# A recurrence step that multiplies by the decay where TensorE left it

## The chip, the cores and the metric

One core of a Trainium2 chip runs the whole program. The metric is device time in microseconds (us), from the core's own record of an execution; lower is better. The engines are TensorE (PE, with its weight loads as PEld), VectorE (DVE), ScalarE (ACT), GpSimd (POOL) and SyncE (SP), which only issues DMAs here.

## The reference

The input `x` is 4 batches of 1024 tokens with 256 channels. It is layer-normed to `xn`, and two parts work on `xn`:

```python
# state-space part: per batch a state h of 256 channels x 16 states
dA = exp(soft_clamp(dt * A)); dB = dt * B            # dt, B, C: projections of xn
h = dA[t] * h + dB[t] * x[t]
h = h * min(20 / norm(h), 1)                          # norm over the whole state of a batch
s[t] = einsum('bdn,bn->bd', h, C[t]) + Dp * x[t]
# expert part: 8 experts, top 2 of each token, capacity 1280
f = combine(gelu(dispatch(xn) @ c_fc) @ c_proj)
out = x + s * silu(f)
```

All of it is float32. The recurrence is serial over 1024 tokens; the expert part is two large matrix products per expert and does not depend on the recurrence.

## The kernel before

**The serial part.** The state of all batches is one tile of 128 partitions by 128 columns. VectorE runs 1024 steps (lines 715 to 756). A step is seven instructions: the state before times the decay (L722, writes `vv`), the clamp of the last norm (L725), two products with a sum (L728, L736), a reduction over partitions (L740), the new state (L751) and a short scan for the next norm (L755). GpSimd takes a power (L531) between L725 and L751. The code counts a step's products in the semaphore `v_ready`.

**What feeds it.** Four steps are a quad, 16 steps (four quads) a block, 64 steps (four blocks) one half of the buffer `tanhb`, which holds the decays with the state index on partitions. For each quad TensorE transposes four slices of `tanhb` into one accumulation bank, `ps[0]` or `ps[1]` by turns (L1170). ScalarE copies the bank to `da`, a ring of 32 steps, eight quads (L952), and counts it in `da_done`; TensorE waits for that copy before it writes the bank again. TensorE then spreads the scan's input with four selection products per quad into `ps[2]` (L1176, "pick"), and ScalarE scales them into `ur`, a ring of the same length (L959, counted in `u_done`). VectorE waits in the last step of each quad, before L736, for the next quad's `ur`; ScalarE's order makes `da` of that quad older than its `ur`. In the first step of a block, before L736, it waits for that block's `output` (L1134 and L1138), which reads the states of two blocks earlier and frees their ring places.

**What lies between.** TensorE and ScalarE each run one fixed order, written out by quad. Behind the transposes and picks of a quad TensorE does the expert work that a list gives to this quad (quads 39 to 229): "up" pieces (L1188, 8 records each), "down" pieces (L1204, 16 records each) and "turn" (L1115); quad 108 has an up and a down, as have quads 91, 177 and 220. In the second quad of a block it does `output` before the transposes. ScalarE does the Gelu of each up piece, and in every quad a share of the tanh of the next half (L858). At the last quad of a half TensorE computes the time rates of a later half (L1059), then one small turn (L1121); ScalarE copies that (L905), changes its function table (L1011) and takes the exponential of the first two quarters of the next half's decays (L864, two of 1.9 us). TensorE waits for the first of these before the next block's first transposes. In the first quad of the new half ScalarE spreads the output weights (L913), makes `da` and `ur`, takes the exponential of the other two quarters, and computes logarithms (L817 to L824). I call this passage, from the last quad of a half into the second quad of the next, a head. There is one at quads 16, 32, 48, ..., 240.

**What runs ahead.** The rings let ScalarE be up to two blocks ahead of VectorE. Nothing ties TensorE's two decay banks to VectorE; TensorE is ahead as far as `output` of the block allows, about five to eight quads.

Of the kernel before, what the change touches and what calls it, by code (L numbers as in the profile page):

```python
# [18 lines left out]
NB, NT, D, NS = 4, 1024, 256, 16  # L19
NE, CAP, FF = 8, 1280, 1024  # L20
P = 128
# [6 lines left out]
BLK = 16  # L28
NBLK = NT // BLK
BPB = P // BLK  # L30
QUAD = 4
QPB = BLK // QUAD
RING = 2 * BLK
# [18 lines left out]
def build(nc, x, wdtT, bdt, wb, wc, a_log, dpar, w_g, c_fc, c_proj, out):  # L52
# [4 lines left out]
    with ctx:  # L57
# [44 lines left out]
        SD = NB * DH * HALF  # L102
        tanhb = take(2 * P * HALF).rearrange("p (f s t) -> p f s t", f=2, t=HALF)
        stage = take(2 * 2 * SD).rearrange("p (f w s) -> p f w s", f=2, w=2)
        da = take(RING * P).rearrange("p (t d) -> p t d", d=P)
        ur = take(RING * P).rearrange("p (t d) -> p t d", d=P)
        hr_at = at[0]
        hr = take(RING * P).rearrange("p (t d) -> p t d", d=P)
# [139 lines left out]
        s_ready = sem("s_ready")  # L248
        ac_ready = sem("ac_ready")
        ta_ps = sem("ta_ps")  # L250
        da_done = sem("da_done")
        tu_ps = sem("tu_ps")
        u_done = sem("u_done")
        be_stage = sem("be_stage")
# [315 lines left out]
        def _(dve):  # L570
# [141 lines left out]

            dve.wait_ge(s_ready, BLK)
            dve.wait_ge(u_done, 2)
            for m in range(CH):
                for k in range(P):
                    slot, before = k % RING, (k - 1) % RING
                    now = m * P + (k + 1 + BLK)
                    step = m * P + k

                    dve.wait_ge(h_ready, now)
                    v.tensor_tensor(vv, hr[:, before, :], da[:, slot, :], ALU.mult).then_inc(v_ready, 1)  # L722

                    dve.wait_ge(q_ready, now)
                    v.tensor_scalar(mx, qv, 1.0, None, ALU.max).then_inc(m_ready, 1)  # L725

                    dve.wait_ge(v_ready, now)
                    v.tensor_tensor_reduce(out=junk[:, 0, :], in0=vv, in1=ur[:, slot, :], scale=2.0 / CLAMP ** 2, scalar=0.0,  # L728
                                           op0=ALU.mult, op1=ALU.add, accum_out=ac[:, 1:2])
                    if k % QUAD == QUAD - 1:  # L730

                        dve.wait_ge(u_done, m * (P // QUAD) + (k // QUAD + 3))
                    elif k % BLK == 0:

                        dve.wait_ge(y_done, m * BPB + (k // BLK + 2))
                    v.tensor_tensor_reduce(out=junk[:, 1, :], in0=vv, in1=vv, scale=1.0 / CLAMP ** 2, scalar=0.0,  # L736
                                           op0=ALU.mult, op1=ALU.add, accum_out=ac[:, 0:1]).then_inc(ac_ready, 1)

                    dve.wait_ge(ac_ready, now)
                    v.tensor_reduce(out=terms[:, slot, 0:2], in_=ac.unsqueeze(2).broadcast_to([P, 2, 32]), axis=AX.X, op=ALU.add,  # L740
                                    apply_transpose=True).then_inc(T_ready, 1)

                    if step in sum_at:
                        add_all_logs(sum_at[step][0])
                    elif step in input_at:
                        half_scan_input(*input_at[step])
                    elif step in norm_at:
                        norm_of_input(norm_at[step][0])

                    dve.wait_ge(s_ready, now)  # L750
                    v.scalar_tensor_tensor(hr[:, slot, :], vv, sv[:, before, 1:2], ur[:, slot, :], ALU.mult, ALU.add)\  # L751
                        .then_inc(h_ready, 1)

                    dve.wait_ge(T_ready, now)
                    v.tensor_tensor_scan(horner, sv[:, before, 1:2].broadcast_to([P, 2]), terms[:, slot, 1:3], terms[:, slot, 0:1],  # L755
                                         ALU.mult, ALU.add).then_inc(q_ready, 1)
# [24 lines left out]
        def _(act):  # L781
# [111 lines left out]
            a.activation(pw[:, 3, :], pw[:, 0, :], ACT.Exp).then_inc(gap_exp, 1)  # L893
            act.wait_ge(lg_ps, 1)
            act.wait_ge(xT_out, 16 * (CH - 1))
            act.sem_inc(da_done, 2)
            act.sem_inc(u_done, 1)
            act.sem_inc(gelu_done, 2)
            act.sem_inc(ye_sb, 1)
# [36 lines left out]
            for blk in range(NBLK):  # L936
# [7 lines left out]
                for q in range(QPB):  # L944
# [3 lines left out]
                        windows(blk)  # L948
                    if q == 1:
                        y_out_of_psum(blk)  # L950
                    act.wait_ge(ta_ps, quad + 2)
                    a.activation(da[:, t:t + QUAD, :].rearrange("p t d -> p (t d)"), ps[q % 2][:, :], ACT.Copy)\  # L952
                        .then_inc(da_done, 1)

                    if q == 0:
                        act.wait_ge(be_stage, blk + 1)
                    act.wait_ge(tu_ps, quad + 1)
# [74 lines left out]
        def _(pe):  # L1032
# [126 lines left out]
            for blk in range(NBLK):  # L1159
                f = blk // 4 % 2  # L1160
                pe.wait_ge(decay_ready, blk + 1)
                for q in range(QPB):
                    quad = blk * QPB + q
                    if q == 1:
                        output(blk, max(1, blk) * BLK + 1, blk % 2)

                    pe.wait_ge(da_done, quad + 1)
                    for j in range(QUAD):
                        s = (blk % 4) * BLK + q * QUAD + j
                        last = t.transpose(ps[q % 2][:, j * P:(j + 1) * P], tanhb[:, f, :, s], ident[:, :])  # L1170
                    last.then_inc(ta_ps, 1)
                    pe.wait_ge(u_done, quad + 1)
                    if q == 0:
                        pe.wait_ge(x_sb, blk + 1)
                    for j in range(QUAD):
                        last = t.matmul(ps[2][:, j * P:(j + 1) * P], pick[:, q * QUAD + j, :], xin, start=True, stop=True)  # L1176
                    last.then_inc(tu_ps, 1)
                    for kind, i, j, _ in by_quad[quad]:
                        if kind == "up":

                            if j == 0:
                                if i % TPE == 0:
                                    pe.wait_ge(wf_in, i // TPE * 16 + 16)
                                pe.wait_ge(xt_in, i + 1)
                            pe.wait_ge(gelu_done, i * FC // 2 + j + 1)
                            for c in range(2):
                                for k in range(DH):
                                    last = t.matmul(ps[4 + j % 2][:, c * TS:(c + 1) * TS],  # L1188
                                                    wf[:, k, (2 * j + c) * P:(2 * j + c + 1) * P], xt[:, k, :],
                                                    start=k == 0, stop=k == DH - 1)  # L1190
                            last.then_inc(mm1_ps, 1)
                        elif kind == "turn":
                            pe.wait_ge(xrow_in, 16 * (i + 1))
                            after_evictions()
                            turn_rows().then_inc(xt_tp, 1)
                            turns = i + 1
                        else:
                            if j == 0:
                                if i % TPE == 0:
                                    pe.wait_ge(wp_in, i // TPE * 16 + 16)  # L1200
                                pe.wait_ge(gelu_done, (i + 1) * FC // 2 + 2)
                                pe.wait_ge(ye_sb, i + 1)
                            for k in range(FC):
                                last = t.matmul(ps[7][:, j * D:(j + 1) * D], hid[:, k, j * P:(j + 1) * P], wp[:, k, :],  # L1204
                                                start=k == 0, stop=k == FC - 1)
                            last.then_inc(mm2_ps, 1)
                    if 0 <= quad - COMBINE_AT < 2 * CH:
                        combine(quad - COMBINE_AT)
                    h = {(3, 3): blk // 4 + 3, (0, 1): blk // 4 + 2, (1, 0): blk // 4 + 1}.get((blk % 4, q), 0)
                    if blk == 0:  # L1210
                        h = {1: 2, 2: 2}.get(q, 0)
                    if 2 <= h < HALVES:
                        if turns:
                            pe.wait_ge(xt_in, turns)
                        after_evictions()
                        if blk % 4 == 3 or (blk == 0 and q == 1):
                            pe.wait_ge(xch_in[h // 2 % 2], 16 * ((h // 2 + 1) // 2))
                            time_rates(h, 6)
                            waiting = [z_used, h + 1]
                        elif blk % 4 == 0:  # L1220
                            b_and_c(h, 6)
                            waiting = [bc_used, h + 1]
                        else:
                            sums_of_squares(h, 6)
                            waiting = [sums_ready, h + 1]

                pe.wait_ge(y_sb, blk + 1)
                if blk + 1 < NBLK:
                    if blk % 4 == 3:
                        pe.wait_ge(du_ready, 4 * (blk // 4 + 2))  # L1230
                    turn_inputs((blk + 1) // 4 % 2, (blk + 1) % 4).then_inc(x_ps, 1)
# [40 lines left out]
```

## Time and profile before

| | us |
|---|---|
| median of 2 runs (1683.84 and 1686.05) | 1684.94 |
| profiled execution, span | 1682.3 |
| DVE busy in it | 1549.9 (92%) |
| PE busy | 1305.2 (78%) |
| ACT busy | 1211.1 (72%) |
| POOL busy | 769.9 (46%) |

The page gives no other time of the profiled execution than its span, from the first to the last instruction. An engine's busy time counts overlapping instructions once. On VectorE neighbouring instructions overlap by some 80 ns, so the durations of a step's instructions add up to more than the step. The rows below come from the page, from tables of stretches, from groups of instructions by line, and from the instructions in order of time.

### The profile page before, as it was taken

The page shows a single profiled execution, that of the slowest core. Times are in us where ns is not written, and L with a number is a line of the kernel's source. Part 1 is how long each engine was busy: PE and PEld are TensorE (multiplying, and loading weights), DVE is VectorE, ACT ScalarE, POOL GpSimd, SP SyncE. Part 2 cuts the span into 40 slices and gives each one's busy share as a digit, 9 for nine tenths or more (in the row PEclk, how much of TensorE's full clock was granted, in tenths as well). Part 3 has the DMA queues.
Part 4 walks back from the last instruction along what each step waited for, and adds up shares of the span by engine and source line. Part 5 has one row for each costly group of instructions (what it writes and reads, how often), then busy time and mean ns, then how long its engine had stood idle before and what let it go on. Part 6 is the DMA issues. An engine that isn't in the chain of part 4 may idle for free.

```text
span 1682.3 us, 33906 instructions
## 1 busy us (share of the span) xinstructions
PE 1305.2 (78%) x9356; PEld 1145.4 (68%) x9356; DVE 1549.9 (92%) x9454; ACT 1211.1 (72%) x3142; POOL 769.9 (46%) x1254
## 2 busy tenths in 40 slices
PE   5864524398979898998989798898979799945661
PEld 5753424387868787787878687797868688834551
DVE  6688888899999999999999999999999989987788
ACT  3695737468877887868787877878777777947551
POOL 3156666543434444443434444343434334468852
PEclk8576767699989999999999999898999999967885
DMA  9941111210111021011002002011101210012245
GB/s 332 338 138 44 45 41 45 84 44 25 50 52 39 25 77 33 18 56 57 27 27 87 25 29 74 25 39 43 57 19 35 66 32 21 20 39 75 73 135 204
DMA packets 95532, 113.28 MB, mean 67 GB/s; under 512 B 8432, under 2 KB 85360, under 8 KB 95344
## 3 DMA queue, kind: packets, MB, share of 16 engines
q1 hardware_dynamic: 87696, 94.13, 17.4%
q0 software_dynamic: 6144, 16.79, 3.1%
q8 instruction: 74, 1.21, 0.3%
q14 instruction: 114, 0.93, 0.2%
q10 hardware_dynamic: 1504, 0.22, 0.1%
HBM read 60.91 MB, written 50.20 MB: 66 GB/s over the span
## 4 chain that ended last, share of the span: by engine, by line
PE 51%; ACT 15%; DVE 14%; POOL 7%; issue 7%; DMA 4%; SPq 1%; POOLq 0%; ACTq 0%; DVEq 0%
PE ps L1204 14%; PE ps L1188 13%; PE ps L1176 9%; PE ps L1170 5%; ACT arena L864 4%; POOL arena L531 4%; DVE arena L751 3%; POOL xg L511 3%; PE ps L1154 3%; PE ps L1138 3%; DVE arena L722 2%; DVE arena L728 2%; ACT arena L858 2%; DVE arena L740 2%; ACT arena L959 2%
## 5 line engine op out<-in xcount | busy, mean ns | idle before, releaser
L531 POOL TENSOR_TENSOR arena<-arena,neghalf 128x1 f32<-128x1 f32 x1025 | 591.3, 577 | 831.6 <-DVE arena L725 759.9
L751 DVE SCALAR_TENSOR_TENSOR arena<-arena 128x128 f32<-128x128 f32 x1024 | 362.6, 354 | 55.8 <-POOL arena L531 55.7
L1176 PE MATMUL ps<-arena,pick 128*128 128x128 f32 x2048 | 302.5, 295 | 48.7 <-ACT arena L959 28.3
L1188 PE MATMUL ps<-arena,wf 128*128 128x256 f32 x1280 | 309.6, 393 | 21.9 <-ACT arena L972 13.8
L1176 PEld LDWEIGHTS ps<-arena,pick 128*128 128x128 f32 x2048 | 279.3, 211 | 62.4 <-ACT arena L959 47.6
L959 ACT ACTIVATE arena<-ps,arena 128x128 f32<-128x128 f32 x1024 | 291.4, 376 | 30.5 <-PE ps L1176 28.8
L736 DVE CUSTOM_DVE_ANT_0 arena<-arena 128x128 f32<-128x128 f32 x1024 | 294.3, 287 | 8.0 <-PE ps L1138 6.5
L1204 PE MATMUL ps<-wp,arena 128*128 128x256 f32 x1280 | 297.3, 386 | 5.0 <-issue 2.7
L728 DVE CUSTOM_DVE_ANT_0 arena<-arena 128x128 f32<-128x128 f32 x1024 | 299.0, 292 | 0.0
L722 DVE TENSOR_TENSOR arena<-arena 128x128 f32<-128x128 f32 x1024 | 290.7, 284 | 0.0
L740 DVE TRANSPOSE_TENSOR_REDUCE arena<-arena 128x2 f32<-128x64 f32 x1024 | 251.3, 245 | 35.5
L1188 PEld LDWEIGHTS ps<-arena,wf 128*128 128x128 f32 x1280 | 245.1, 198 | 55.4 <-ACT arena L972 14.8
L858 ACT ACTIVATE arena<-arena,a16c,a 128x256 f32<-128x256 f32 x512 | 278.7, 609 | 0.1
L1204 PEld LDWEIGHTS ps<-wp,arena 128*128 128x128 f32 x1280 | 243.0, 195 | 36.7 <-issue 2.9
L1170 PE MATMUL ps<-ident,arena 128*128 128x128 f32 x1024 | 209.3, 331 | 59.6 <-ACT arena L864 58.8
L1170 PEld LDWEIGHTS ps<-ident,arena 128*128 128x128 f32 x1024 | 179.7, 244 | 89.0 <-ACT arena L864 64.8
L755 DVE TENSOR_TENSOR_SCAN arena<-arena 128x2 f32<-128x2 f32 x1024 | 221.1, 216 | 0.0
L952 ACT ACTIVATE arena<-ps 128x512 f32<-128x512 f32 x256 | 152.2, 595 | 70.8 <-PE ps L1170 61.4
L725 DVE TENSOR_SCALAR arena<-arena 128x1 f32<-128x1 f32 x1024 | 150.3, 147 | 0.0
L972 ACT ACTIVATE arena<-ps 128x512 f32<-128x512 f32 x160 | 95.4, 608 | 66.7 <-PE ps L1188 64.4
L913 ACT ACTIVATE arena<-arena,winmask 128x16 f32<-128x16 f32 x520 | 110.9, 316 | 21.2 <-POOL arena L538 21.0
L864 ACT ACTIVATE arena<-arena 128x2048 f32<-128x2048 f32 x64 | 119.0, 1907 | 0.2
(145 smaller groups left out, 1292.6 us busy)
## 6 DMA issues: line engine op xcount, KB each, us to landing
xg<-zeros SPq DMA_DIRECT2D x10, 1024.0 KB, 9.6
xrow<-xg SPq DMA_DIRECT2D x40, 256.0 KB, 2.8
yg<-arena SPq DMA_DIRECT2D x40, 256.0 KB, 2.2
arena<-in_x SPq DMA_DIRECT2D x16, 512.0 KB, 9.5
wf<-in_c_fc SPq DMA_DIRECT2D x8, 1024.0 KB, 5.0
wp<-in_c_proj SPq DMA_DIRECT2D x8, 1024.0 KB, 5.9
arena<-dx SPq DMA_DIRECT2D x66, 64.0 KB
ys<-arena SPq DMA_DIRECT2D x66, 64.0 KB
```

What stands on the lines that cost most here:

```text
L531: g.tensor_tensor(sv[:, slot, 1:2], mx, neghalf[:, 0:1], ALU.pow).then_inc(s_ready, 1)
L722: v.tensor_tensor(vv, hr[:, before, :], da[:, slot, :], ALU.mult).then_inc(v_ready, 1)
L728: v.tensor_tensor_reduce(out=junk[:, 0, :], in0=vv, in1=ur[:, slot, :], scale=2.0 / CLAMP ** 2, scalar=0.0, op0=ALU.mult, op1=ALU.add, acc ...
L736: v.tensor_tensor_reduce(out=junk[:, 1, :], in0=vv, in1=vv, scale=1.0 / CLAMP ** 2, scalar=0.0, op0=ALU.mult, op1=ALU.add, accum_out=ac[:, ...
L740: v.tensor_reduce(out=terms[:, slot, 0:2], in_=ac.unsqueeze(2).broadcast_to([P, 2, 32]), axis=AX.X, op=ALU.add, apply_transpose=True).then ...
L751: v.scalar_tensor_tensor(hr[:, slot, :], vv, sv[:, before, 1:2], ur[:, slot, :], ALU.mult, ALU.add)\
L858: last = a.activation(dst[:, :, k, n_, :], src[:, :, k, :], ACT.Tanh, scale=a16[:, c:c + 1], bias=a16c[:, c:c + 1])
L959: last = a.activation(ur[:, t + j, :], ps[2][:, j * P:(j + 1) * P], ACT.Copy, scale=terms[:, t + j, 3:4])
L1170: last = t.transpose(ps[q % 2][:, j * P:(j + 1) * P], tanhb[:, f, :, s], ident[:, :])
L1176: last = t.matmul(ps[2][:, j * P:(j + 1) * P], pick[:, q * QUAD + j, :], xin, start=True, stop=True)
L1188: last = t.matmul(ps[4 + j % 2][:, c * TS:(c + 1) * TS], wf[:, k, (2 * j + c) * P:(2 * j + c + 1) * P], xt[:, k, :], start=k == 0, stop=k ...
L1204: last = t.matmul(ps[7][:, j * D:(j + 1) * D], hid[:, k, j * P:(j + 1) * P], wp[:, k, :], start=k == 0, stop=k == FC - 1)
```

## The change

VectorE's product L722 reads the decay from the accumulation bank in place of the ring `da`. ScalarE's copy L952 goes, with the semaphore `da_done`. TensorE writes a bank again when VectorE has done the products of the quad that was in it: before the transposes of a quad it waits until the products of all steps up to two quads back are counted in `v_ready`. VectorE waits for the transposes (`ta_ps`) of the next quad in the third step of each quad, before L736. The space of `da` stays allocated, so that no other buffer moves.

```diff
-        da = take(RING * P).rearrange("p (t d) -> p t d", d=P)
+        take(RING * P)
...
             dve.wait_ge(u_done, 2)
+            dve.wait_ge(ta_ps, 2)
...
-                    v.tensor_tensor(vv, hr[:, before, :], da[:, slot, :], ALU.mult).then_inc(v_ready, 1)
+                    v.tensor_tensor(vv, hr[:, before, :], ps[k // QUAD % 2][:, k % QUAD * P:(k % QUAD + 1) * P], ALU.mult).then_inc(v_ready, 1)
...
                     if k % QUAD == QUAD - 1:
 
                         dve.wait_ge(u_done, m * (P // QUAD) + (k // QUAD + 3))
+                    elif k % QUAD == QUAD - 2 and step < NT - QUAD:
+
+                        dve.wait_ge(ta_ps, m * (P // QUAD) + (k // QUAD + 3))
...
-            act.sem_inc(da_done, 2)
...
-                    act.wait_ge(ta_ps, quad + 2)
-                    a.activation(da[:, t:t + QUAD, :].rearrange("p t d -> p (t d)"), ps[q % 2][:, :], ACT.Copy)\
-                        .then_inc(da_done, 1)
-
...
-                    pe.wait_ge(da_done, quad + 1)
+                    if quad >= 2:
+                        pe.wait_ge(v_ready, BLK + QUAD * (quad - 1))
                     for j in range(QUAD):
```

`v_ready` starts at `BLK` (16), so the wait before quad n's transposes asks for the products of 4(n-1) steps.

## Rows read from the trace of the kernel before

**Rows 1.** The page: the span, and each engine's busy time, share and instructions.

```profile
span 1682.3 us, 33906 instructions
PE 1305.2 (78%) x9356; PEld 1145.4 (68%) x9356; DVE 1549.9 (92%) x9454; ACT 1211.1 (72%) x3142; POOL 769.9 (46%) x1254
```

**Rows 2.** Stretches: us, busy time of each engine (instructions), granted clock, DMA, GB/s.

```profile
340.00:1490.00 1150.00, 1032.15 (x7452) 912.63 (x7451) 1117.84 (x7070) 916.99 (x2367) 462.78 (x829) 0.95 0.13 40
1400.00:1500.00 100.00, 79.21 (x582) 69.80 (x580) 96.66 (x614) 81.30 (x218) 43.78 (x75) 0.90 0.08 23
200.00:300.00 100.00, 43.24 (x330) 37.09 (x328) 84.87 (x515) 57.86 (x152) 63.41 (x89) 0.69 0.13 44
```

**Rows 3.** Instructions in order of time on all engines, one step: start, duration, what.

```profile
802.23 0.29 DVE L722 TENSOR_TENSOR arena<-arena 128x128 f32<-128x128 f32 x1
...
802.78 0.29 DVE L736 CUSTOM_DVE_ANT_0 arena<-arena 128x128 f32<-128x128 f32 x1
...
803.69 0.28 DVE L722 TENSOR_TENSOR arena<-arena 128x128 f32<-128x128 f32 x1
```

**Rows 4.** Waits over the whole span: who for whom, us in total, times, longest.

```profile
ACT arena L952 <- PE ps L1170: 61.4, 53, 13.3
...
DVE arena L751 <- POOL arena L531: 55.7, 132, 1.8
...
DVE arena L736 <- PE ps L1138: 6.5, 4, 3.5
...
DVE arena L736 <- ACT arena L959: 1.5, 4, 0.6
```

**Rows 5.** VectorE's groups by line and shape: count, busy us, mean ns, idle before.

```profile
L722 DVE TENSOR_TENSOR arena<-arena 128x128 f32<-128x128 f32 x1024 | 290.7, 284 | 0.0
...
L700 DVE TENSOR_TENSOR wp<-wp 128x512 f32<-128x512 f32 x1 | 0.7, 693 | 0.0
...
L701 DVE TENSOR_TENSOR wp<-wp,ps 128x512 f32<-128x512 f32 x1 | 0.7, 689 | 0.0
...
L675 DVE COPY arena<-ps 128x256 f32<-128x256 f32 x1 | 0.4, 425 | 4.9 <-PE ps L1051 4.9
...
L671 DVE CAST arena<-arena 128x256 f32<-128x256 int32 x1 | 0.3, 285 | 0.0
```

**Rows 6.** VectorE in order of time: the first products of quads 78 to 81.

```profile
580.38 0.28 DVE L722 TENSOR_TENSOR arena<-arena 128x128 f32<-128x128 f32 x1
...
586.14 0.29 DVE L722 TENSOR_TENSOR arena<-arena 128x128 f32<-128x128 f32 x1
...
591.93 0.28 DVE L722 TENSOR_TENSOR arena<-arena 128x128 f32<-128x128 f32 x1
...
598.31 0.28 DVE L722 TENSOR_TENSOR arena<-arena 128x128 f32<-128x128 f32 x1
```

**Rows 7.** TensorE in order of time: transposes of quads 79 and 80.

```profile
568.14 0.71 PE L1170 MATMUL ps<-ident,arena 128*128 128x128 f32 x4
...
578.65 1.02 PE L1170 MATMUL ps<-ident,arena 128*128 128x128 f32 x4 [3.59 <-ACT arena L864]
```

**Rows 8.** ScalarE in order of time: the head at quad 80.

```profile
576.68 3.71 ACT L864 ACTIVATE arena<-arena 128x2048 f32<-128x2048 f32 x2
...
582.00 0.57 ACT L952 ACTIVATE arena<-ps 128x512 f32<-128x512 f32 x1
582.48 1.11 ACT L959 ACTIVATE arena<-ps,arena 128x128 f32<-128x128 f32 x4
583.48 3.71 ACT L864 ACTIVATE arena<-arena 128x2048 f32<-128x2048 f32 x2
...
592.93 1.11 ACT L959 ACTIVATE arena<-ps,arena 128x128 f32<-128x128 f32 x4
```

**Rows 9.** TensorE in order of time: quad 108 and the output behind it.

```profile
736.87 0.75 PE L1170 MATMUL ps<-ident,arena 128*128 128x128 f32 x4
...
748.52 1.08 PE L1138 MATMUL ps<-arena 128*32 128x128 f32 x32
```

More of the change, by code:

```diff
@@ L250, in build @@
         ta_ps = sem("ta_ps")
-        da_done = sem("da_done")
         tu_ps = sem("tu_ps")
```

## The prediction, made before the changed kernel was run

> **What bounds the kernel now.** I read the page's busy line first: VectorE is busy 92% of a span of 1682.3 us [rows 1]. The table of stretches says where: from 340 to 1490 us, the stretch of the expert work, VectorE is busy 1118 of 1150 us, TensorE 1032 and ScalarE 917 [rows 2]. The instructions in order of time show a step: 1.45 us from one L722 to the next [rows 3], so a quad is 5.77 us (580.38 to 586.14, [rows 6]) and 1024 steps are about 1480 us. The list of waits shows VectorE losing almost nothing to those who feed it: 6.5 us to TensorE's output, 1.5 us to ScalarE's `ur`; the 55.7 us on GpSimd's power lie outside the change [rows 4]. So the recurrence is the bound, and the copy L952, 0.57 us a quad [rows 8], is not on its path.
>
> What hides all other work is distance. TensorE transposed quad 79 at 568.14 and VectorE began on it at 586.14: 18 us ahead [rows 6, 7]. The `ur` of quad 80 was ready at 583.59 for a start at 591.93, that of quad 81 at 594.04 for 598.31 [rows 6, 8]. The lead shrinks by several us in a head, where ScalarE does long exponentials and logarithms, and is won back in the quads after it. The question is what the change does to that lead.
>
> **The product from the bank.** The trace has one VectorE product with an operand in a bank: L701 took 689 ns at 512 columns, against 693 for the same operation from plain memory, L700 [rows 5]. So per step the price is about nothing, -4 ns at the low end (-4 us in 1024 steps). The high end is from a farther pair: the copy L675 out of a bank took 425 ns for 256 columns, a cast from memory of the same size, L671, 285 [rows 5]: +140 ns, 143 us in all. I take 0, since L701 has the same operation and type. The Trainium skill says otherwise ("VectorE: DVE Perf Modes", section "The TRN2 errata"): it gives a VectorE operation 58 cycles plus its columns from plain memory and 120 from a bank at 0.96 GHz, which would by estimate be 65 ns a step and 66 us in all. L701's row disagrees with that; it is one row, so the price stays as a rival.
>
> **The copy that goes.** It was never waited for by VectorE; ScalarE loses 0.48 us of its sequence per quad (582.00 to 582.48, [rows 8]) and its waits for transposes (61.4 us, [rows 4]). That is worth at most the 1.5 us that VectorE waited for ScalarE: -1 us. It does shorten the chains below, and I subtract it there.
>
> **TensorE's new wait.** Before, a bank came free with ScalarE's copy, which could run blocks ahead. Now the transposes of quad n wait until VectorE has done the last product of quad n-2, one step before quad n-1 begins: at its start, less 1.45, plus 0.28 for the product and some 0.08 to get across, that is 1.08 us before quad n-1 starts. TensorE's lead is then at most 5.77 + 1.08 = 6.85 us, where it was 18. All of TensorE's order is queued behind this wait: the picks of that quad, its expert pieces, the turn, the output of the block. ScalarE's `ur` follows the picks, so the ring of eight quads in `ur` can no longer be filled either. I price this at a head and in the quads between.
>
> **A head, first half.** From the transposes of quad 79 (568.14) to the end of `ur` of quad 80 (582.48 + 1.11 = 583.59) is a chain of 15.45 us [rows 7, 8]: TensorE's quad and time rates, the table change, the exponential for which TensorE idled 3.59 us [rows 7], the second one, the windows, `ur`. Without the copy it is 14.97. What VectorE now allows: the transposes of quad 79 may start 1.08 us before quad 78 starts, and `ur` of quad 80 is due at L736 of the last step of quad 79, which is 5.77 + 3 x 1.44 + 0.55 = 10.65 us after that start (L736 stands 0.55 behind L722, [rows 3]). So 11.73 us are allowed, and VectorE stalls 3.2 us.
>
> **A head, second half.** From that `ur` to the `ur` of quad 81 (592.93 + 1.11 = 594.04) ScalarE needs 10.45 us, 9.97 without the copy: two more exponentials, 3.71 us, then logarithms, a table change, tanh [rows 8]. It arrives just in time at the first, so only VectorE's own quad covers it, 6.38 us here (591.93 to 598.31, [rows 6]). VectorE stalls 3.6 us more: 6.8 a head. Before, the same passage used up lead (18.0 us of TensorE's, then 4.27 us left of `ur`'s) and cost nothing.
>
> There are twelve heads in the expert stretch (quads 48 to 224): 82 us. The first follows a quad without expert pieces and the last has no logarithms any more; I take 3 off for each: 76 us. The three others (quads 16, 32 and 240) have longer quads, since GpSimd holds the steps up there; bounded by 0 and 3.6, I take 2 each: 6 us.
>
> **Between the heads.** TensorE wins its 6.85 us back soon, as a quad of its work is on average under 5.77 (1032 us of 1150). Where a quad is heavy the small lead breaks: at quad 108 the output ends 12.73 us after the transposes (736.87 to 749.60, [rows 9]), 12.25 without the copy, and may end 1.08 + 5.77 + 0.55 = 7.40 after; 4.9 us of stall. Three other quads have such a pair of pieces, two of them beside a head, which hides a part; with small dips at block starts I take 12 us, between 5 and 25. VectorE's third-step wait for transposes is met wherever the one for `ur` is, as picks and `ur` come after them; price 0.
>
> **TensorE's clock.** The same work in a longer stretch makes TensorE less busy: 1032 of some 1240 us, 83%. Rows with a busy share of 79% and 43% had a granted clock of 0.90 and 0.69, the whole expert stretch with 90% had 0.95 [rows 2]; these are means over its two levels, 1.2 and 2.4 GHz. At about 0.92 TensorE's 7 us of a head grow by 3%, with small dips 3 us in all; bounds 0 and 15.
>
> **SP and the end.** SP loads the last operands when the last transposes are done, which is now up to 6 us later against the loop's end; they were 18 us early, so nothing is due. No DMA is added or removed.
>
> Sum: 76 + 6 + 12 + 3 - 1 + 0 = 96 us on 1682.3, so 1778. The two runs shown have a median 2.6 us above the profiled span; I predict **1781**.
>
> **The rivals.**
> *The bank costs time as well.* Condition: L722 longer than its 284 ns, or L728 later behind it. At 70 ns, half of the high bound, 1024 steps cost 72 us; a quad longer by 0.28 gives the heads some 0.7 us each back, 8 in all: 1781 + 64 = 1845. L701 speaks against it. With the 65 ns that the Trainium skill's page would give it would be some 1840. Chance 0.14.
> *TensorE becomes the bound.* If the pauses at the heads lower the granted clock for long, 1032 us at 0.95 become 1153 at 0.85, the whole stretch before, and every dip stalls VectorE: another 60 us, about 1840; at the 0.69 of the early stretch it would be 1421 us, +271. For it: the early row. Against: the pauses for L864 are there already, and the stretch has 0.95. Chance 0.08.
> *The lead was not needed (the other side).* If ScalarE, rid of 256 copies, starts its head work that much earlier, and head chains of 15 and 10 us shrink below 11.73 and 6.38, VectorE never waits, and the time is the old one less up to 8 us of waits: 1677 to 1685. It decides at 3.2 and 3.6 us of shortening per half; the copy gives 0.5 each. For it: ScalarE is 80% busy and idles between Gelus. Against: in the head it runs back to back, with nothing to pull forward. Chance 0.09.
> *A faster step.* Over 2% would need L722 33 ns shorter; L701 shows 4 of 693. Chance 0.02.
> My forecast keeps 0.67.
>
> **How the numbers follow.** 2% of 1685 is 34 us, about what a measurement tells from no change: 1651 to 1719. The forecast's own range is 1740 to 1815: half a stall per head at one end (-40), the upper bounds of the dips and the clock at the other (+25, and rounding). The range reaches to the bank's price and to the mild clock case: 1738 to 1845, leaving out the unchanged time and the deep clock fall. Slower: 0.67 + 0.14 + 0.08, less 0.02 for stalls much smaller than worked out, 0.87. Same: 0.09 + 0.02 = 0.11. Faster: 0.02.
>
> **What will show it.** Right: L722 stays near 284 ns; in the list of waits VectorE's L736 waits for L959 and L1138 together by some 90 us in 25 to 40 places, 6 to 8 us at each head; TensorE's L1170 waits for VectorE's L722; TensorE's transposes stand at most 7 us before their quad's first product. The bank's price would show as a step over 1.45 us in quiet quads; the clock as a value under 0.9 between 340 and 1490 us. Wrong altogether would be a step pitch of 1.45 through the heads.

## The result

The changed kernel is slower: 1803.26 us (median of 2 runs, 1800.11 and 1806.42) against 1684.94, a ratio of 1.0712 [1.0693, 1.073]. The forecast was slower, 1781 us, range 1738 to 1845. The profiled execution is the longer of the two runs.

The page after: VectorE is as long at work as before, in a span that is 121.8 us longer [rows 1].

```profile
span 1804.1 us, 33649 instructions
PE 1361.4 (75%) x9356; PEld 1177.5 (65%) x9356; DVE 1546.8 (86%) x9454; ACT 1093.5 (61%) x2886; POOL 769.7 (43%) x1254
```

VectorE's groups after (idle time before them, and what ended it, behind the second bar): the product now has `ps` among its inputs and takes 280 ns, where it took 284 [rows 5]. The idle time stands before the second product with a sum (L736 before, L739 now), where VectorE's three waits for TensorE and ScalarE are.

```profile
L739 DVE CUSTOM_DVE_ANT_0 arena<-arena 128x128 f32<-128x128 f32 x1024 | 295.0, 288 | 131.9 <-ACT arena L957 61.4
...
L722 DVE TENSOR_TENSOR arena<-arena,ps 128x128 f32<-128x128 f32 x1024 | 286.8, 280 | 0.0
```

The list of waits after (us in total, times, longest) gives 61.4 + 54.2 + 16.0 = 131.6 us where it gave 8.0 [rows 4], and TensorE's transposes wait 242 us for VectorE's product, which they never did:

```profile
PE ps L1169 <- DVE arena L722: 242.3, 122, 6.0
...
DVE arena L739 <- ACT arena L957: 61.4, 30, 4.6
...
DVE arena L739 <- PE ps L1136: 54.2, 25, 7.4
...
DVE arena L739 <- PE ps L1169: 16.0, 11, 2.2
```

All 11 waits for the transposes (L1169) stand in the third step of a quad whose last step then waits for `ur` as well, which comes later.

The head at quad 80, VectorE in order of time (the numbers in brackets are idle time and its releaser). Quads 79 and 80 last 8.88 and 10.58 us (from one L722 to the next, 607.69, 616.57, 627.15), where they lasted 5.79 and 6.38 [rows 6].

```profile
607.69 0.28 DVE L722 TENSOR_TENSOR arena<-arena,ps 128x128 f32<-128x128 f32 x1
...
612.10 0.29 DVE L739 CUSTOM_DVE_ANT_0 arena<-arena 128x128 f32<-128x128 f32 x1 [0.91 <-PE ps L1169]
...
615.71 0.29 DVE L739 CUSTOM_DVE_ANT_0 arena<-arena 128x128 f32<-128x128 f32 x1 [2.13 <-ACT arena L957]
...
616.57 0.28 DVE L722 TENSOR_TENSOR arena<-arena,ps 128x128 f32<-128x128 f32 x1
...
617.71 0.31 DVE L739 CUSTOM_DVE_ANT_0 arena<-arena 128x128 f32<-128x128 f32 x1 [0.52 <-PE ps L1136]
...
625.69 0.29 DVE L739 CUSTOM_DVE_ANT_0 arena<-arena 128x128 f32<-128x128 f32 x1 [3.60 <-ACT arena L957]
...
627.15 0.28 DVE L722 TENSOR_TENSOR arena<-arena,ps 128x128 f32<-128x128 f32 x1
```

TensorE's transposes of quads 79 and 80 in the same head: the first at 600.85, 6.84 us ahead of quad 79's first product at 607.69, where the lead was 18.0 [rows 6, 7]; the second 10.36 us later (10.51 before), again behind the exponential.

```profile
600.85 0.85 PE L1169 MATMUL ps<-ident,arena 128*128 128x128 f32 x4 [1.34 <-DVE arena L722]
...
611.21 0.85 PE L1169 MATMUL ps<-ident,arena 128*128 128x128 f32 x4 [3.59 <-ACT arena L867]
```

ScalarE there: `ur` of quad 80 ends at 615.68 and `ur` of quad 81 at 625.65, 9.97 us later; each time VectorE's L739 starts 0.03 to 0.04 us behind it.

```profile
614.57 1.11 ACT L957 ACTIVATE arena<-ps,arena 128x128 f32<-128x128 f32 x4
615.57 3.71 ACT L867 ACTIVATE arena<-arena 128x2048 f32<-128x2048 f32 x2
...
624.52 1.13 ACT L957 ACTIVATE arena<-ps,arena 128x128 f32<-128x128 f32 x4
```

Where the 121.8 us went, from the start of every quad's first product in both traces: the twelve heads of the expert stretch 91.4 (first halves 36.9, second halves 54.5), the three others 10.9, all other quads 19.4. A first half is here the last quad of a half of `tanhb`, a second half the two quads behind it.

### The profile page after: what moved, and what is told of

It reads as the page before. It is cut to its first block, busy times and chain, and to the rows that moved or that the text cites. A ratio compares the mean times of both kernels' runs of the same rounds, so it can differ in the third digit from the quotient of the medians.

```text
span 1804.1 us, 33649 instructions
## 1 busy us (share of the span) xinstructions
PE 1361.4 (75%) x9356; PEld 1177.5 (65%) x9356; DVE 1546.8 (86%) x9454; ACT 1093.5 (61%) x2886; POOL 769.7 (43%) x1254
## 4 chain that ended last, share of the span: by engine, by line
DVE 48%; PE 20%; ACT 14%; POOL 8%; issue 6%; DMA 3%; SPq 0%; POOLq 0%; ACTq 0%; DVEq 0%
DVE arena L754 9%; DVE arena L728 8%; DVE arena L743 7%; DVE arena L739 7%; DVE arena L722 7%; ACT arena L867 5%; PE ps L1203 5%; DVE arena L758 4%; POOL arena L530 4%; PE ps L1175 3%; PE ps L1187 3%; PE ps L1169 2%; POOL xg L510 2%; DVE arena L725 2%; PE ps L1057 2%
## 5 line engine op out<-in xcount | busy, mean ns | idle before, releaser
L1169 PE MATMUL ps<-ident,arena 128*128 128x128 f32 x1024 | 230.5, 355 | 296.6 <-DVE arena L722 242.3
L1169 PEld LDWEIGHTS ps<-ident,arena 128*128 128x128 f32 x1024 | 177.3, 244 | 361.5 <-DVE arena L722 208.8
L739 DVE CUSTOM_DVE_ANT_0 arena<-arena 128x128 f32<-128x128 f32 x1024 | 295.0, 288 | 131.9 <-ACT arena L957 61.4
L1175 PE MATMUL ps<-arena,pick 128*128 128x128 f32 x2048 | 330.4, 314 | 10.7 <-ACT arena L957 7.4
L1187 PE MATMUL ps<-arena,wf 128*128 128x256 f32 x1280 | 315.5, 398 | 15.7 <-ACT arena L970 9.4
L1175 PEld LDWEIGHTS ps<-arena,pick 128*128 128x128 f32 x2048 | 312.4, 232 | 13.6 <-ACT arena L957 8.5
L1203 PE MATMUL ps<-wp,arena 128*128 128x256 f32 x1280 | 302.3, 391 | 3.7 <-issue 3.0
L728 DVE CUSTOM_DVE_ANT_0 arena<-arena 128x128 f32<-128x128 f32 x1024 | 299.1, 292 | 0.0
L722 DVE TENSOR_TENSOR arena<-arena,ps 128x128 f32<-128x128 f32 x1024 | 286.8, 280 | 0.0
L1187 PEld LDWEIGHTS ps<-arena,wf 128*128 128x128 f32 x1280 | 250.4, 203 | 50.9 <-ACT arena L970 10.4
L1203 PEld LDWEIGHTS ps<-wp,arena 128*128 128x128 f32 x1280 | 247.2, 199 | 37.0 <-issue 3.3
L970 ACT ACTIVATE arena<-ps 128x512 f32<-128x512 f32 x160 | 95.2, 600 | 100.8 <-PE ps L1187 100.3
L867 ACT ACTIVATE arena<-arena 128x2048 f32<-128x2048 f32 x64 | 118.9, 1904 | 0.2
L728 DVE DVE_READ_ACCUMULATOR2_ANT arena<- 128x1 f32 x1024 | 83.7, 82 | 0.0
```

The source lines that it names most:

```text
L722: v.tensor_tensor(vv, hr[:, before, :], ps[k // QUAD % 2][:, k % QUAD * P:(k % QUAD + 1) * P], ALU.mult).then_inc(v_ready, 1)
L1187: last = t.matmul(ps[4 + j % 2][:, c * TS:(c + 1) * TS], wf[:, k, (2 * j + c) * P:(2 * j + c + 1) * P], xt[:, k, :], start=k == 0, stop=k ...
```

## The experiments

The theory: the bank's reuse on VectorE's signal shortens the lead of all that TensorE and ScalarE do for the recurrence, and a head then stalls VectorE. The rivals: the read from the bank or VectorE's new wait is what costs; the copy was worth something in itself; TensorE's clock is lower. Medians are of four or five executions in three rounds, beside runs of the kernel before on the same chip, which had medians of 1682 to 1684 us. The changed kernel's 1803.26 us is the median of its two executions above.

**The copy kept, the lead cut.** VectorE reads the ring `da` as before; TensorE alone gets the change's wait.

```diff
                     pe.wait_ge(da_done, quad + 1)
+                    if quad >= 2:
+                        pe.wait_ge(v_ready, BLK + QUAD * (quad - 1))
```

> The kernel before with one line added: TensorE waits, besides ScalarE's copy, until VectorE has done the products of two quads back. VectorE still reads the ring da. Theory (the small lead is the loss, the read from the bank is free): as slow as the changed kernel and a little slower, since the copy's 0.48 us stays in both halves of each head: 1803 plus 12 x 1.0 plus 2 for L722's 284 against 280 ns, so 1810 to 1822 us. Rival (the bank's read, or VectorE's own new wait, is the loss): both are gone here, so 1683 to 1700 us.

Measured: 1834.44 us, ratio 1.0892 [1.0861, 1.0922]. There is no read from a bank and no new wait on VectorE here, and all of the loss and more. VectorE's waits:

```profile
DVE arena L736 <- ACT arena L959: 101.9, 37, 5.1
DVE arena L736 <- PE ps L1138: 55.9, 21, 8.2
```

So the wait on TensorE alone does it. The expectation was 12 us or more too low: the heads of the expert stretch cost 102.2 us against 91.4 (+11, as worked out), but the other three cost 6 more and the quads between 12 more. Of that some 4 are L722's 284 ns against 280; that the copy makes the rest, because it stands in every chain that is now tight, is argued and not shown place by place. This kernel is 31 us slower than the changed one. Less the product's 4, the copy's removal is worth some 27 us under the small lead.

**The lead held to three quads, and to four.** The same with the wait one and two quads further back.

```diff
-                    if quad >= 2:
-                        pe.wait_ge(v_ready, BLK + QUAD * (quad - 1))
+                    if quad >= 3:                                        # four: quad >= 4
+                        pe.wait_ge(v_ready, BLK + QUAD * (quad - 2))     # four: (quad - 3)
```

> As the kernel with the copy kept and TensorE held to two quads (1834 us), but held to three: TensorE's lead is at most 12.6 us. Theory: the first half of a head (15.45 us against 17.5 allowed) costs nothing, and 2 us are left over; of the second half (10.5 to 11 less 5.83) about 2.9 us stay at each head: 35 us, with the rest 30 to 50 us on the kernel before: 1715 to 1735 us. Rival (the wait as such, one more semaphore for TensorE, costs it): still above 1800 us.

> Held to four quads, a lead of at most 18.4 us, about what the kernel before had at quad 79 (18.0). Theory: the stalls are gone but for places where the kernel before had them too: 1684 to 1695 us. Rival (the wait as such): above 1800 us.

Measured: 1724.64 us (ratio 1.0248 [1.0229, 1.0267]) and 1688.56 us (1.0041 [1.0024, 1.0059]). VectorE's waits with three quads, then with four:

```profile
DVE arena L736 <- PE ps L1138: 25.6, 7, 5.9
DVE arena L736 <- ACT arena L959: 22.1, 10, 3.7
```

```profile
DVE arena L736 <- PE ps L1138: 5.1, 2, 3.0
DVE arena L736 <- ACT arena L959: 2.7, 2, 2.5
```

The same wait, with the same count on the same engine, costs 150, 42 or 6 us by how far back it asks. Held to three, the first halves of the heads cost nothing and the second halves 26 us, 2.2 on average, for the 2.9 worked out. Held to four, VectorE waits for TensorE and ScalarE no longer than before (7.8 us for 8.0 [rows 4]), so four quads (a lead of at most 18.4 us) are enough for a head, and three (12.6) are not. Where the 6 us that are left went, these waits do not show. The same kernel answers for the clock: its mean granted clock over the whole execution was 0.862, as low as the changed kernel's 0.861 (0.874 before), and it lost only these 6 us.

**Shorter exponentials in the head.** The last two quarters' exponentials cut.

```diff
-                part = tanhb[:, f, :, c * BLK:(c + 1) * BLK]
+                part = tanhb[:, f, :, c * BLK:c * BLK + (BLK if c < 2 else 1)]
```

> The changed kernel with the exponentials of the last two quarters of each half cut from 2048 to 128 columns; the decays of those steps are left without their exponential. ScalarE's second chain of a head shrinks from 9.98 us by some 3.2 us. Theory (the second half of a head is ScalarE's chain against 5.83 us of VectorE's): 3.2 us less at each of 12 heads and up to 3 at the three others, 38 to 48 us: 1755 to 1768 us. Rival (the stall is TensorE's output or transposes there): under 15 us less, 1788 us or more.

Measured: 1771.40 us, 32 us less than the changed kernel; its span is 36 us shorter. That is somewhat less than expected. The second halves of the twelve heads went from 54.5 to 21.0 us and the first halves stayed at 36.9, which is the pattern of the theory; each second half gave 2.8 us for the 3.2 taken out. In the list of waits ScalarE's share nearly halves, from 61.4 us, and that of TensorE's output is 46.7 for 54.2.

```profile
DVE arena L739 <- PE ps L1136: 46.7, 26, 5.3
DVE arena L739 <- ACT arena L957: 34.1, 22, 3.0
```

At quads 96, 112 and 128 VectorE now waits mostly or only for the output: the waits for it grow from 0.47, 1.82 and 0.52 us to 1.49, 3.26 and 1.81. At quads 160 and 208 they shrink from 7.1 to 2.7 us, so the output was late there because of ScalarE's head too.

**Giving the work a longer lead with the same two banks.** TensorE's order is changed: the transposes of a quad, with the wait for VectorE's products and the one for ScalarE's exponentials ahead of them, come behind the picks and the expert pieces of the same quad (first kernel) or of the next quad (second kernel).

```diff
-                    if quad >= 2:
-                        pe.wait_ge(v_ready, BLK + QUAD * (quad - 1))
-                    for j in range(QUAD): ...transposes...
                     pe.wait_ge(u_done, quad + 1)
                     ...picks, expert pieces, rates...
+                    decays(quad)          # the waits and the transposes; second kernel: decays(quad - 1)
```

> The changed kernel with TensorE's transposes of a quad, and the wait ahead of them, moved behind the picks, the expert pieces and the rates of the same quad. That work then stands one quad, 5.77 us, earlier against VectorE; nothing else changes. Theory: the first half of a head (3.4 us) vanishes, of the second half (4.2 us) about 2 us stay: 24 to 35 us of stall over 15 heads plus a few between, 1705 to 1735 us. Rival (any order is as slow, because the bank's read or the waits themselves cost it): 1795 to 1810 us.

> As the one with the transposes behind their quad's work, but the transposes of a quad stand behind the work of the next quad, so picks, scan inputs and expert pieces run one more quad (5.77 us) ahead. Theory: the rest of the head's stalls goes too, 1684 to 1702 us; no gain on the kernel before beyond L722's 4 ns a step and the 8 us that VectorE waited, 1677 us at best, since VectorE's steps are the bound. Rival (the freed ScalarE is worth more): below 1670 us. Rival (transposes now come late, their window is 4.6 us): 1720 us or more with VectorE's L736 waiting for the transposes.

Measured: 1773.45 us (ratio 1.0534 [1.0507, 1.0561]) and 1783.07 us (1.0593 [1.0567, 1.0619]). Both theories missed: 30 and 20 us came back, where 68 or more and 101 or more were expected. For the second kernel its last rival came true, 1720 us or more with VectorE waiting for the transposes. VectorE's waits in the first kernel say why. `ur` is no longer late, 5.8 us for 61.4, as the theory has it; the transposes are.

```profile
DVE arena L739 <- PE ps L1162: 97.5, 32, 10.7
...
DVE arena L739 <- ACT arena L957: 5.8, 3, 2.5
```

In order of time at quad 97, TensorE first, then ScalarE and VectorE: an up piece (L1189) waits 3.40 us for a Gelu (L970) that stands behind ScalarE's exponentials (L867) and logarithms (L827 the last of them), the small products of L1067 follow, then the transposes, and VectorE has waited 7.96 us.

```profile
703.92 1.89 PE L1189 MATMUL ps<-arena,wf 128*128 128x256 f32 x8
709.22 2.66 PE L1189 MATMUL ps<-arena,wf 128*128 128x256 f32 x8 [3.40 <-ACT arena L970]
...
712.84 1.13 PE L1162 MATMUL ps<-ident,arena 128*128 128x128 f32 x4
```

```profile
700.78 3.71 ACT L867 ACTIVATE arena<-arena 128x2048 f32<-128x2048 f32 x2
...
706.62 0.63 ACT L827 ACTIVATE arena<-arena 128x512 f32<-128x512 f32 x1
...
708.57 0.60 ACT L970 ACTIVATE arena<-ps 128x512 f32<-128x512 f32 x1
```

```profile
714.00 0.29 DVE L739 CUSTOM_DVE_ANT_0 arena<-arena 128x128 f32<-128x128 f32 x1 [7.96 <-PE ps L1162]
```

The move gave the work a lead and put ScalarE's head in front of the decays. The second kernel has the same wait, 103.7 us in 28 places, one quad earlier at most heads.

**The same, but transposes ahead of the work in the first two quads of a half.**

```diff
+                    if quad % 16 < 2:
+                        decays(quad)
                     pe.wait_ge(u_done, quad + 1)
                     ...picks, expert pieces, rates...
-                    decays(quad)
+                    if quad % 16 >= 2:
+                        decays(quad)
```

> The changed kernel with the transposes behind their quad's work, except in the first two quads of each half, where they stand ahead of it as in the changed kernel. In the order with all transposes behind (1773 us) VectorE waited 97 us for transposes that stood behind up pieces, which waited for a Gelu behind ScalarE's exponentials and logarithms. Theory (lead for the work, and nothing of ScalarE's head between VectorE and its decays): about 2 us a head stay and little else, 1705 to 1735 us. Rival (no order within two banks helps): 1765 us or more.

Measured: 1747.35 us, ratio 1.0388 [1.0371, 1.0405]: 56 us of the 118 come back, between the theory's upper end (1735) and the rival's 1765. In the twelve heads and between them, first halves and the other quads now cost under 3 us together, but the second halves still 48.5; the three other heads cost 11.0. VectorE's waits:

```profile
DVE arena L739 <- PE ps L1162: 32.9, 25, 4.3
...
DVE arena L739 <- PE ps L1136: 26.5, 9, 5.8
...
DVE arena L739 <- ACT arena L957: 17.1, 8, 2.8
```

Of the 48.5 us, 15 stand in the second quad of the half, where VectorE waits for the transposes of the third, which come behind their quad's work again. At quad 80 TensorE has nothing left to do before the transposes and waits for VectorE's product, so that the picks behind it, and the output, lose the quad that was won:

```profile
596.96 1.13 PE L1162 MATMUL ps<-ident,arena 128*128 128x128 f32 x4 [4.81 <-DVE arena L722]
```

In each of the four orders tried with two banks, something of a head still stands behind VectorE's signal. Whether another order would win the rest was not tried, nor a kernel in which VectorE reads the bank and TensorE has more than two: that a longer lead gives the time back is shown with the copy kept.

**What the copy is worth with the lead intact.** The kernel before, its copy cut to 4 columns.

```diff
-                    a.activation(da[:, t:t + QUAD, :].rearrange("p t d -> p (t d)"), ps[q % 2][:, :], ACT.Copy)\
+                    a.activation(da[:, t, 0:4], ps[q % 2][:, 0:4], ACT.Copy)\
```

> The kernel before with ScalarE's copy of a bank cut from 512 columns to 4; VectorE reads what lies in the ring, so the decays are left out, all waits stay. Theory (with the lead intact the copy is hidden, so its removal is worth nothing): 1676 to 1686 us, at most the 8 us that VectorE waited for ScalarE and TensorE. Rival (the copy is on the path, and the change pays it back in part): 0.3 us in 256 quads, 77 us less: below 1640 us.

Measured: 1676.35 us against 1683.37, ratio 0.995 [0.9933, 0.9967], within what was expected: most of the 8.0 us that VectorE had waited [rows 4], of which 2.2 are left. That is about all there was to win from a shorter copy.

## Why the prediction was right, step by step

- **The product from the bank**: taken at 0, bounds -4 and +143 us. It is at the low end: 280 for 284 ns in 1024 instructions, about 4 us won. L701's one row told it rightly. The next product, L728, has 292 ns in both kernels. The difference between the Trainium skill's fixed costs of 58 cycles from plain memory and 120 from a bank ("VectorE: DVE Perf Modes", section "The TRN2 errata") does not show here: the measured product is no longer, and the kernel with the copy kept is slower, not faster. The rival in which the bank costs time is out.
- **TensorE's lead**: worked out as 6.85 us at most, measured 6.84 at quad 79 and up to 6.86 in the last quads of the other halves of the expert stretch. Behind a stall it reads longer, up to 11.5, because the stall itself delays the product. The lead before was not 18 us throughout, nor five to eight quads: in the last quads of the halves it was 14 to 21 us, on average over quads 40 to 235 12.9, and behind some heads 4 to 6.
- **A head, first half**: 3.2 us worked out, 3.1 at quad 79 and mostly 3.4 elsewhere, from 0 at quad 47 to 4.4 at quad 127; 36.9 us over the twelve heads, against 12 x 3.2 less 3, 36. The chain took 14.83 us at quad 79 (600.85 to 615.68) for the 14.97 worked out. The rival in which the lead was not needed is out: neither chain came under what VectorE allows.
- **A head, second half**: mis-sized. 3.6 us were worked out, 4.2 came at quad 80; over the twelve 54.5 us against 12 x 3.6 less 3, 40. The chain on ScalarE was exact, 9.97 us. What I set against it was the length of quad 80 from its first product to the next quad's, 6.38 us. But the wait stands at L736, and from L736 in the last step of quad 79 to L736 in the last step of quad 80 the kernel before had 5.83 us:

```profile
591.02 0.28 DVE L736 CUSTOM_DVE_ANT_0 arena<-arena 128x128 f32<-128x128 f32 x1
...
596.85 0.29 DVE L736 CUSTOM_DVE_ANT_0 arena<-arena 128x128 f32<-128x128 f32 x1
```

  The half microsecond that makes this quad long lies behind the wait, in the same step, and covers nothing. 9.97 less 5.83 is 4.14. The same slip is in the 4.27 us that the prediction says were left of `ur`'s lead: it was due at 596.85, 2.81 us after 594.04. Heads with up pieces have a Gelu or two more in that chain and came to 4.7 to 5.2. At quads 160 and 208 the output stands behind a turn, which waits for ScalarE's L822 ahead of the logarithms, and VectorE waits 7.1 us for it (at quad 208 it had waited 3.5 before). The sum had priced the output at quad 108 alone.
- **The other three heads**: 10.9 us, not 6; at quad 240 alone 6.4, where I had capped it at 3.6 from ScalarE's chain; VectorE waits 7.4 there for the output.
- **Between the heads**: 12 us taken, bounds 5 and 25; 19.4 net of the product's 4, so some 23. Quad 108 lost 3.4 for the 4.9 worked out. Of the three other quads with such a pair only 177 lies in a head, and it lost nothing; 91 and 220 lost 1.7 and 2.5. The rest are many small places, at block starts above all.
- **VectorE's wait for the transposes**: priced at 0. It took 16.0 us in the list, each time in a quad that then waits for `ur` too. That `ur`'s wait would otherwise have been that much longer follows from the order and was not tested.
- **The copy that goes**: -1 us taken in all, beside its part in the chains. With the lead intact a copy of 4 columns won 7 us, as VectorE's waits for TensorE's output shrank too, which I had not counted. Under the small lead some 27 us were the copy's, which I had counted only in the heads and at quad 108.
- **TensorE's clock**: 0.94 over the first 1150 us of the stretch, for 0.95 before [rows 2] and the 0.92 that I took; the rival in which it falls (under 0.9) did not come. These are means over its two levels, 1.2 and 2.4 GHz. From 340 to 1610 us, about where the same work now ends, it was 0.94 too, so my 0.92 was too low.

```profile
340.00:1490.00 1150.00, 980.62 (x6824) 849.22 (x6825) 1019.60 (x6456) 757.77 (x1979) 422.63 (x757) 0.94 0.13 39
```

- **The signs**: L739 waited for `ur` and the output together 115.6 us in 55 places, where I had some 90 in 25 to 40; a head of the expert stretch cost 4.9 to 9.8 us, for 6 to 8. A step in quiet quads was 1.446 us, so neither the bank's price nor a faster step of over 2% came.

The two steps that fell short, second halves and small dips, make up 14 and 11 of the 26 us between 96 and 122. The three other heads add 5; the product takes 4 back, and the 3 set aside for the clock do not show.

## What to carry to other kernels

A copy out of an accumulation bank is also a queue: before taking it out, count by how many pieces of work it lets the producer run ahead, and hold that against the longest passage in which the producer, or whoever follows it in the same order, is busy with something else. Here the copy cost 0.5 us a quad off the path and allowed 14 to 21 us of lead ahead of a head, where 12.6 at most was too little and 18.4 at most was enough. When a wait is priced, measure the cover from wait to wait, not from one start of the piece of work to the next.

## What the runs showed of the hardware that was not expected

VectorE's product with one operand in a bank took 280 ns, 4 less than with both in plain memory. It was as short while other engines used other banks: by the trace's starts and ends it took 281.8 ns in the 68 steps in which TensorE's transposes wrote the other bank, 279.5 in the 215 in which ScalarE read a third, and 280.1 in the rest; no step had both. The step became shorter by the same 4 ns, 1.463 us against 1.467 on average over quads 71 to 76, block start included.
